# Bias rows of the second FFN as split bf16, residual loads on two queues, and a reordered entry of the first attention

## The chip, the cores and the metric

The kernel runs on one core of one Trainium2 chip. The metric is the device time of one execution in microseconds (us). TensorE is called PE here, VectorE DVE, ScalarE ACT, GpSimd POOL and SyncE SP, as in the profile.

## The reference

Six stages follow each other over a residual `x` of 8 batches x 512 tokens x 256 features, in float32:

```python
x = x + 0.5 * _L0_ffn_ref(_layernorm(x), ...)   # f0: 64 experts, top 3, capacity 128
x = x + _L0_attn_ref(_layernorm(x), ...)        # a0: windowed attention, window 32
x = x + 0.5 * _L0_ffn_ref(_layernorm(x), ...)   # f0
x = x + 0.5 * _L1_ffn_ref(_layernorm(x), ...)   # f1: 8 experts, all computed, top 2 weighted
x = x + _L1_attn_ref(_layernorm(x), ...)        # a1: causal attention
x = x + 0.5 * _L1_ffn_ref(_layernorm(x), ...)   # f1
```

The bias that the change touches is that of the second layer's FFN:

```python
y = jnp.einsum('bseh,ehd->bsed', h, W2) + b2
expert_out = jnp.einsum('bse,bsed->bsd', gate_full, y)
shared = jax.nn.gelu(x @ Ws1 + bs1, approximate=False) @ Ws2 + bs2
```

The sum over the experts of gate x `b2` is a product of its own: gates (tokens x 9, the ninth column is the shared expert's constant) times bias rows (9 x 256).

In a0, each pair of a token and one of its 32 window places gives a bond term and a damage term, both through a GELU; small 16x16 matrices (`w_state`, `w_strain`, ...) act on every head, and a mean over the window is taken with a banded matrix.

## The kernel before

The residual stays in SBUF as `x_resid`. `macaron` (L2692) runs `load_phase` and then the six stages; each stage is one block with a program per engine, and between stages all engines meet at a barrier (L51). A stage's first instructions therefore start about 1 us after the last engine has finished the stage before.

**Residual loads.** `load_x` (L54) issues eight DMAs of 512 KB, one per batch, on SP's queue: at the start of the kernel from `x`, and at the end of each f0 from the scratch `acc_rows` (L1576), once every expert's rows have been added (`y_added`). Each batch has a semaphore of its own (`wait_x`). After its loads `load_phase` writes zeros to scratch memory on the same queue (L88).

**Second FFN (f1, L186).** Per batch of 512 tokens, `up` (L293) makes the hidden layer of an expert (2 matmuls of 512 columns), ACT applies the GELU, `down` (L303) makes four token tiles of 256 columns, and DVE adds each tile, scaled by the gate, to the residual (`add`, L413). There are 9 such rounds n, one for each expert; four banks `y_ps` are used in turn, and `y_free` keeps PE from overtaking DVE by more than two rounds. Beside that, for the batch that follows: statistics at n = 0, normalised rows at n = 2, transposes at n = 4 and 5, gate logits at n = 6, and the gates themselves on DVE (`gates`, L381) at n = 7. At n = 2 PE turns the gates (9 rows) and DVE copies them to `gate_t` (L411). After the ninth round `biases` (L317) makes four matmuls with the 9 gate rows as weights and `b2_sb` (9 x 256, float32) as the moving side (L324); DVE adds the result as a tenth round. Before the loop over pairs of batches PE waits for `up_loaded` and `down_loaded` (L333), and DVE has computed `gates(0, 0)`. The biases are loaded by two DMAs (L257, L258).

**First attention (a0, L1712).** A batch is 16 chunks of 4 window places x 8 heads. For each chunk DVE makes `bond_buf` (`bond_chunk`, four instructions, L2411) and POOL `dmg_buf` (`damage_chunk`, L2062); ACT applies a GELU to each (L2336, L2341), PE reduces both. Three buffers of each kind are used in turn. Token work of the next batch is spread over the 16 steps. Only the first batch's token work and the matrices made of weights stand ahead of the loop; this is the entry that the change reorders. In the kernel before it runs as follows. SP issues 12 small loads (L1955 to L1963), then eight larger ones. DVE starts with the statistics of batch 0, waits for the small loads (L2575), spreads them with PE's help over heads (L2253, L2578, L2583), copies the transposed tokens (L2517) and goes on alternately with displacement tiles, the banded matrices (from L2606; they wait for POOL's constants, the last of which is an iota at L2052), statistics of the other batches, `split_bias` (L2498, seven small operations that turn the output bias into three bf16 rows), means, and the biases (`biases_ready`, L2632). PE makes q, a and c (L2237 to L2249) for the first half; `copy_c` (L2544) releases POOL's first chunk, and `bond_chunk(0)` ACT's first GELU.

Of the kernel before, what the change touches and what calls it, by code (L numbers as in the profile page):

```python
# [26 lines left out]
class Core:  # L27
# [26 lines left out]
    def load_x(self, sp, rows):  # L54
        for i in range(B):
            sp.dma_start(self.x_batch(i), rows[i * S:(i + 1) * S, :].rearrange("(j p) d -> p j d", p=P)).then_inc(
                self.x_loaded[i], 16)
        self.x_loads += 1
# [12 lines left out]
def load_phase(core, x_dram, scratch):  # L71
# [3 lines left out]
    with ExitStack() as ctx:  # L75
        zeroed = core.semaphore("zeroed")
        spare_zeroed = core.semaphore("spare_zeroed")
        block = ctx.enter_context(nc.Block())

        @block.sync  # L80
        def _(sp):
            core.load_x(sp, x_dram.rearrange("b s d -> (b s) d"))
# [9 lines left out]
        def _(pool):  # L92
# [6 lines left out]
                                    fill=1.0, base=0, pattern=[[-1, P]], channel_multiplier=1)  # L99

# [85 lines left out]
def ffn1_phase(core, name, gate_w, w1, b1, w2, b2, ws1, bs1, ws2, bs2, route_scale, out_dram=None):  # L186

    nc = core.nc  # L190
# [4 lines left out]
    YB = 4  # L195
    ctx = ExitStack()
    with ctx:
# [8 lines left out]
        b2_sb = sb("b2", [NE, D])  # L206
# [11 lines left out]
        gate_t = [sb(f"gate_t{k}", [NE, S]) for k in range(2)]  # L218
# [11 lines left out]
        const_ready = sem("const_ready")  # L230
        logits_ready = sem("logits_ready")
        sig_ready = sem("sig_ready")
        gate_ready = sem("gate_ready")
# [11 lines left out]
        def _(sp):  # L245
# [11 lines left out]
            sp.dma_start(b2_sb[0:E, :], b2).then_inc(down_loaded, 16)  # L257
            sp.dma_start(b2_sb[E:NE, :], bs2.rearrange("(o d) -> o d", o=1)).then_inc(down_loaded, 16)  # L258
# [7 lines left out]
        def _(pool):  # L266
            nc.gpsimd.iota(iota_e[:, :, :], pattern=[[0, TPB], [1, E]], base=0, channel_multiplier=0,
# [6 lines left out]
        def _(pe):  # L274
# [11 lines left out]
            def turn_gates(i, k):  # L286
                pe.wait_ge(gate_ready, i + 1)
                for j in range(TPB):
                    last = nc.tensor.transpose(gate_ps[0:NE, j * P:(j + 1) * P], gate[k][:, j, :],  # L289
                                               core.ident[:, :])  # L290
                last.then_inc(gate_t_ready, 1)
# [42 lines left out]
            pe.wait_ge(down_loaded, 64)  # L334
            with pe.Fori(0, B // 2) as pair:
                for k in range(2):
                    i = pair * 2 + k
                    for n in range(NE):
# [3 lines left out]
                        if n == 2:  # L342
                            turn_gates(i, k)
# [36 lines left out]
        def _(dve):  # L380
            def gates(i, k):  # L381
# [20 lines left out]
                for r in range(2):  # L402
# [4 lines left out]
                                        ALU.add).then_inc(gate_ready, 1)  # L407

            def copy_gates(i, k):
# [2342 lines left out]
```

## Time and profile before

| | |
|---|---|
| median of 3 runs | 3161.79 us (3155.25 to 3163.49) |
| the profiled execution | 3150.57 us, its span 3148.8 us |
| PE busy | 2839.0 us, 90% of the span |
| DVE / ACT / POOL busy | 53% / 49% / 41% |
| mean granted PE clock | 0.952 |

The stages can be told by their lines: f0 from 13 to 620 us and from 1339 to 1938 us, a0 from 629 to 1338, f1 from 1947 to about 2264 and from 2835 to the end, a1 in between. Read first the chain that ended last, for the stage at the end; then the busy time by stretches, for each stage's bound; then the timeline at the places that the change touches. A row of the timeline gives start, duration of the run of instructions, engine, line, operation, out<-in and count; in brackets stands the idle time ahead of it and what ended it. "issue" there is time in which the engine waited for nothing that the profile shows.

### The profile page before, as it was taken

How to read it: one execution, taken by the hardware profiler on the slowest of the kernel's cores; microseconds unless marked ns; L12 is line 12 of the kernel's file. 1: busy time of each engine (PE TensorE's matmuls, PEld its weight loads, DVE VectorE, ACT ScalarE, POOL GpSimd, SP SyncE). 2: the span in 40 equal slices, each digit the busy share in tenths (PEclk: the TensorE clock that was granted, in tenths of full speed). 3: DMA queues.
4: the chain of work that ended last, by engine and by line, in shares of the span. 5: the costliest groups of instructions: out<-in, count | busy, mean ns of one | idle time of the engine just before them, and what ended most of it. 6: DMA issues, size and time to landing. Idle time of an engine off the chain costs nothing. (4 is left out here: it accounts for less than half of the span.)

```text
span 3148.8 us, 54094 instructions
## 1 busy us (share of the span) xinstructions
PE 2839.0 (90%) x19481; PEld 2042.4 (65%) x19481; DVE 1666.4 (53%) x4549; ACT 1539.0 (49%) x2605; POOL 1306.5 (41%) x1303
## 2 busy tenths in 40 slices
PE   4899999758889988678999997999879999989999
PEld 3799999733344443358999996666546666655666
DVE  4411111178888888463111111666676666655666
ACT  1133333239999998311333332333257777772333
POOL 3544444349998889254444442000044444320000
PEclk9899999979999999868999998999989999998999
DMA  8199999711655555752999996000152344201000
GB/s 284 41 306 327 329 327 325 234 30 18 64 63 62 62 63 62 96 198 86 328 327 326 327 326 203 1 0 0 32 124 72 87 96 101 72 1 38 13 13 20
DMA packets 359857, 431.97 MB, mean 137 GB/s; under 512 B 86193, under 2 KB 314566, under 8 KB 356550
## 3 DMA queue, kind: packets, MB, share of 16 engines
q1 hardware_dynamic: 335046, 395.30, 45.5%
q0 software_dynamic: 24576, 33.57, 5.0%
q8 instruction: 144, 2.36, 0.3%
q14 instruction: 91, 0.75, 0.1%
HBM read 355.93 MB, written 72.88 MB: 136 GB/s over the span
## 5 line engine op out<-in xcount | busy, mean ns | idle before, releaser
L1675 ACT ACTIVATE f_h_t<-f_h_ps,f_b_t 128x128 f32<-128x128 f32 x1024 | 320.2, 364 | 596.3 <-PE f_h_ps L1633 596.3
L2062 POOL TENSOR_TENSOR a_dmg_buf<-a_c 128x2048 f32<-128x2048 f32 x128 | 520.1, 4091 | 85.2 <-DVE a_c L2544 42.7
L1633 PEld LDWEIGHTS f_h_ps<-f_rows_t,f_w 128*128 128x128 f32 x4096 | 481.4, 193 | 9.9 <-issue 3.5
L1633 PE MATMUL f_h_ps<-f_rows_t,f_w 128*128 128x128 f32 x4096 | 482.6, 276 | 2.3 <-DVE f_rows_t L1687 1.2
L1647 PE MATMUL f_y_ps<-f_w,f_h_t 128*128 128x256 f32 x2048 | 483.4, 379 | 0.0
L1593 POOL DMA_INDIRECT acc_rows<-f_y,f_give x128 | 205.1, 1603 | 487.2 <-DMA acc_rows<-f_y,f_give 451.6
L1647 PEld LDWEIGHTS f_y_ps<-f_w,f_h_t 128*128 128x128 f32 x2048 | 369.8, 190 | 39.9
L1687 DVE COPY f_rows_t<-f_t_ps 128x256 f32<-128x256 f32 x128 | 54.4, 425 | 598.4 <-PE f_t_ps L1621 593.7
L2411 DVE SCALAR_TENSOR_TENSOR a_bond_buf<-a_a,a_small_rep,a_q_ps 128x512 f32<-128x512 f32 x512 | 346.8, 740 | 5.3 <-PE a_q_ps L2238 2.2
L428 DVE SCALAR_TENSOR_TENSOR x_resid<-f_y_ps,f_gate,x_resid 128x256 f32 x512 | 218.8, 479 | 161.1 <-PE f_y_ps L311 155.5
L885 ACT ACTIVATE a_prob<-a_prob,a_neg_top 128x384 f32<-128x384 f32 (+3 forms) x512 | 276.5, 569 | 47.9 <-POOL a_neg_top L702 47.7
L299 PE MATMUL f_h_ps<-f_xn_t,f_w 128*128 128x512 f32 x584 | 282.8, 611 | 2.6 <-DVE f_xn_t L176 1.7
L998 DVE CUSTOM_DVE_ANT_0 a_prob<-a_s_ps,a_factor 128x384 f32<-128x384 f32 (+3 forms) x512 | 234.5, 486 | 87.5 <-PE a_s_ps L779 85.6
L360 ACT ACTIVATE f_h_t<-f_h_ps,f_b 128x512 f32<-128x512 f32 x146 | 100.3, 687 | 368.9 <-PE f_h_ps L299 368.6
L311 PEld LDWEIGHTS f_y_ps<-f_w,f_h_t 128*128 128x128 f32 x1152 | 220.1, 191 | 86.6 <-issue 53.7
L311 PE MATMUL f_y_ps<-f_w,f_h_t 128*128 128x256 f32 x1152 | 271.3, 381 | 0.1
L2336 ACT ACTIVATE a_bond_buf<-a_bond_buf,a_bond_act_b 128x2048 f32<-128x2048 f32 x128 | 255.7, 1998 | 16.5 <-DVE a_bond_buf L2411 12.2
L2341 ACT ACTIVATE a_dmg_buf<-a_dmg_buf,a_small_rep 128x2048 f32<-128x2048 f32 x128 | 255.0, 1992 | 0.0
L790 PE MATMUL a_t_ps<-ident,a_prob 128*128 128x128 f32 x1280 | 232.6, 281 | 17.0 <-ACT a_prob_t L896 13.3
L896 ACT COPY a_prob_t<-a_t_ps 128x512 f32<-128x512 f32 (+1 forms) x352 | 192.8, 548 | 100.6 <-PE a_t_ps L790 99.3
L702 POOL TENSOR_SCALAR a_neg_top<-a_top 128x1 f32<-128x1 f32 x512 | 105.8, 211 | 324.4 <-DVE a_top L998 307.1
L790 PEld LDWEIGHTS a_t_ps<-ident,a_prob 128*128 128x128 f32 x1280 | 145.5, 142 | 108.7 <-ACT a_prob L885 47.7
(337 smaller groups left out, 4110.4 us busy)
## 6 DMA issues: line engine op xcount, KB each, us to landing
f_w<-in_L_ffn_w_dram SPq DMA_DIRECT2D x256, 1024.0 KB
a_skewed<-skew SPq DMA_DIRECT2D x32, 512.0 KB, 7.2
a_k_s<-parts SPq DMA_DIRECT2D x16, 768.0 KB, 7.9
acc_rows<-x_resid SPq DMA_DIRECT2D x17, 512.0 KB, 5.3
xn_rows<-f_xn SPq DMA_DIRECT2D x16, 512.0 KB, 3.0
x_resid<-acc_rows SPq DMA_DIRECT2D x16, 512.0 KB, 8.3
a_vals<-val_rows SPq DMA_DIRECT2D x64, 128.0 KB, 4.2
skew<-a_bond SPq DMA_DIRECT2D x128, 64.0 KB
```

The source lines that it names most:

```text
L299: last = nc.tensor.matmul(h_ps[(k * NE + n) % 2][:, :], w1_sb[:, RUN[n], c, :], norm.xn_t[k][:, c, :], start=c == 0, stop=c == DC - 1)
L311: last = nc.tensor.matmul(y_ps[m % YB][:, j, :], h[:, t * P:(t + 1) * P], w2_sb[:, RUN[n], :], start=True, stop=True)
L790: last = nc.tensor.transpose(t_ps[pack % TB][:, col + kb * P:col + (kb + 1) * P], prob[:, u % PR, kb * P:(kb + 1) * P], core.ident[:, :])
L885: nc.scalar.activation(prob[:, u % PR, 0:width], prob[:, u % PR, 0:width], ACT.Exp, bias=neg_top[:, u % PR:u % PR + 1]).then_inc(exp_ready, 1)
L998: nc.vector.tensor_tensor_reduce(out=prob[:, u % PR, 0:width], in0=s_ps[use % SB][:, 0:width], in1=factor[:, S - width:S], scale=1.0, scal ...
L1633: last = nc.tensor.matmul(h_ps[n // HB][:, (n % HB) * P:(n % HB + 1) * P], w1_sb[s][:, c, n * P:(n + 1) * P], rows_t[e % 2][:, c, :], star ...
L1647: last = nc.tensor.matmul(y_ps[k][:, 0:D], h_t[k][:, n, :], w2_sb[e % R][:, n, :], start=n == 0, stop=n == HC - 1)
L1675: nc.scalar.activation(h_t[k][:, n, :], h_ps[n // HB][:, (n % HB) * P:(n % HB + 1) * P], ACT.Gelu, bias=b1_t[:, n, e:e + 1]).then_inc(gelu ...
L2062: nc.gpsimd.tensor_tensor(dmg_buf[n % RING][:, :, :], places(c_sb[h], first_place(dg)), c_sb[h][:, PAD:].unsqueeze(1).broadcast_to([P, DG, ...
L2336: nc.scalar.activation(buf[:, :, :], buf[:, :, :], ACT.Gelu, bias=bond_act_b[:, h:h + 1]).then_inc(bond_act, 1)
L2341: nc.scalar.activation(buf[:, :, :], buf[:, :, :], ACT.Gelu, bias=small_rep[:, B_DAMAGE:B_DAMAGE + 1]).then_inc(dmg_act, 1)
L2411: last = nc.vector.scalar_tensor_tensor(out=bond_buf[n % RING][:, dd, :], in0=a_sb[h][:, d + 1:d + 1 + S], scalar=small_rep[:, POS + d:POS ...
```

## The change

It has four parts.

1. **Second FFN's biases in bf16.** Each float32 bias value is split into three bf16 parts, and so is each gate; the products of every gate part with every bias part are made in one bf16 matmul with 96 rows (three blocks of 32, in each 3 x 9 used rows) in place of a float32 one with 9 rows. The biases are loaded nine times over (18 small DMAs in place of 2), behind a memset on POOL. `split_biases` (8 DVE operations) stands after `gates(0, 0)`, and PE waits for it ahead of its loop. Per batch DVE gets `split_first` (4 operations, n = 0) and `split_second` (2, n = 1); the gates are turned and copied at n = 3, from a single `gate_t` buffer.
2. **Residual loads on two queues.** SP loads the even batches, ACT the odd ones, in `load_phase` and at the end of each f0.
3. **The 12 small loads of a0** are issued in `load_phase`, between the residual loads and the writing of zeros.
4. **a0's entry.** On DVE and PE what depends on weights and constants alone comes first, the banded matrices and their wait for POOL's iota among it; then batch 0's statistics. `make_a` comes ahead of `make_q`, `inverse_std` ahead of `copy_c`; `split_bias` stands after `bond_chunk(0)`; ACT runs one GELU on a single column, right after the second square root.

```diff
+    def load_x(self, queue, rows, batches):
+        for i in batches:
+            queue.dma_start(self.x_batch(i), ...)
...
+        @block.scalar
+        def _(act):
+            core.load_x(act, x_dram.rearrange("b s d -> (b s) d"), range(1, B, 2))
         @block.sync
         def _(sp):
+            core.load_x(sp, x_dram.rearrange("b s d -> (b s) d"), range(0, B, 2))
+            attn0.load(sp)
             sp.wait_ge(spare_zeroed, 1)
...
+            sp.wait_ge(b2_cleared, 1)
+            for m in range(PARTS):
+                for l in range(PARTS):
+                    row = 32 * m + NE * l
+                    sp.dma_start(b2_sb[row:row + E, :], b2).then_inc(b2_loaded, 16)
+                    sp.dma_start(b2_sb[row + E:row + NE, :], bs2.rearrange("(o d) -> o d", o=1)).then_inc(b2_loaded, 16)
...
-                        last = nc.tensor.matmul(y_ps[m % YB][:, j, :], gate_t[k][:, t * P:(t + 1) * P],
-                                                b2_sb[:, :], start=True, stop=True)
+                        last = nc.tensor.matmul(y_ps[m % YB][:, j, :], gate_t[:, t * P:(t + 1) * P],
+                                                b2_rows[:, :], start=True, stop=True)
...
-            pe.wait_ge(down_loaded, 64)
+            pe.wait_ge(down_loaded, 32)
+            pe.wait_ge(b2_split, 1)
...
+            def split_biases():
+                dve.wait_ge(b2_loaded, 32 * PARTS * PARTS)
+                nc.vector.tensor_copy(b2_part[:, :], b2_sb[:, :])
+                nc.vector.drain()
+                nc.vector.tensor_copy(b2_rows[0:32, :], b2_part[0:32, :])
+                nc.vector.tensor_tensor(b2_rest[:, :], b2_sb[:, :], b2_part[:, :], ALU.subtract)
+                nc.vector.drain()
...
+            def split_first(k):
+                nc.vector.tensor_copy(gate_part[0][:, :, :], gate[k][:, :, :])
+                nc.vector.drain()
+                nc.vector.tensor_tensor(gate_rest[:, :, :], gate[k][:, :, :], gate_part[0][:, :, :], ALU.subtract)
+                nc.vector.tensor_copy(place_part(0), across(gate_part[0][:, :, :]))
+                nc.vector.drain()
+                nc.vector.tensor_copy(gate_part[1][:, :, :], gate_rest[:, :, :])
...
             gates(0, 0)
+            split_biases()
...
             sp.wait_ge(y_added, 16 * E)
-            core.load_x(sp, sparse.acc)
+            core.load_x(sp, sparse.acc, range(0, B, 2))
...
+            act.wait_ge(y_added, 16 * E)
+            core.load_x(act, sparse.acc, range(1, B, 2))
...
+            nc.scalar.activation(tanh[:, 0:1], core.ident[:, 0:1], ACT.Gelu)
...
             dve.wait_ge(bands_ready, 1)
...
+            bn_stats(0, 1)
+            aggregate(0, 1)
+            variances(0, 1)
+            inverse_std(0, 1, 1)
...
             copy_a(0, 0)
-            variances(1, B)
+            inverse_std(1, B, 2)
             copy_c(0, 0)
-            inverse_std(1, B, 2)
             dve.wait_ge(pads_ready, 1)
             bond_chunk(0)
+            split_bias()
             for s in range(LAST):
                 if s + 1 < CHUNKS:
                     bond_chunk(s + 1)
```

## Rows read from the trace of the kernel before

**Rows 1.** The chain that ended last, shares of the span by line:

```profile
by line: PE f_h_ps L299 4.1%; PE f_y_ps L311 3.9%; PE f_gate_ps L281 0.5%; PE f_y_ps L324 0.4%; PE f_tp L164 0.3%; PE f_gate_ps L289 0.1%; issue 0.1%; DVE x_resid L428 0.1%; DVE f_xn_t L176 0.0%; DVE f_xn L152 0.0%; DVEq L458 0.0%; DVE f_st
```

**Rows 2.** Busy us by stretch, a0's second batch: stretch, length, PE, PEld, DVE, ACT, POOL:

```profile
765.00:847.00 82.00, 69.41 (x574) 29.44 (x578) 71.57 (x113) 80.41 (x54) 78.97 (x21) 0.98 0.51 59
```

**Rows 3.** Timeline, PE: last f1's bias matmuls and what follows; two bf16 matmuls of a1:

```profile
2994.72 1.99 PE L324 MATMUL f_y_ps<-f_b,f_gate_t 9*128 9x256 f32 x8
2996.64 3.70 PE L299 MATMUL f_h_ps<-f_xn_t,f_w 128*128 128x512 f32 x8
...
2801.07 0.28 PE L777 MATMUL a_s_ps<-a_k_s,a_q_s 96*128 96x256 bf16 x1
2801.19 0.22 PE L779 MATMUL a_s_ps<-a_mask_b,a_ident_b 128*128 128x128 bf16 x1
```

**Rows 4.** Timeline, DVE, last f1: the adds at n = 2 and n = 8:

```profile
2971.92 1.74 DVE L428 SCALAR_TENSOR_TENSOR x_resid<-f_y_ps,f_gate,x_resid 128x256 f32 x4 [1.49 <-PE f_y_ps L311]
...
2996.93 1.66 DVE L428 SCALAR_TENSOR_TENSOR x_resid<-f_y_ps,f_gate,x_resid 128x256 f32 x4 [0.17 <-PE f_y_ps L324]
```

**Rows 5.** Timeline, entry of the last f1:

```profile
2841.96 0.25 SPq L258 DMA_DIRECT2D f_b<-in_L_ffn_bs_dram  x1
2850.51 3.76 PE L299 MATMUL f_h_ps<-f_xn_t,f_w 128*128 128x512 f32 x4
2854.36 2.87 PE L311 MATMUL f_y_ps<-f_w,f_h_t 128*128 128x256 f32 x8
2855.04 0.19 DVE L406 TENSOR_TENSOR f_gate<-f_part 128x32 f32<-128x32 f32 x1
```

**Rows 6.** Timeline, DVE: first and last of the seven operations of a0's `split_bias`:

```profile
656.47 0.27 DVE L2501 CAST a_b_out_part<-a_b_out 3x256 bf16<-3x256 f32 x1
...
658.81 0.47 DVE L2512 SCALAR_TENSOR_TENSOR a_b_out_rows<-a_ctx,ident,a_ctx_t 3x256 bf16<-3x256 f32 x1
```

**Rows 7.** Timeline, entry of the first f1:

```profile
1963.54 3.78 PE L299 MATMUL f_h_ps<-f_xn_t,f_w 128*128 128x512 f32 x4 [0.86 <-DMA f_b<-in_L_ffn_bs_dram]
1967.07 0.19 DVE L406 TENSOR_TENSOR f_gate<-f_part 128x32 f32<-128x32 f32 x1
```

**Rows 8.** Timeline, SP: first two and last of eight residual loads; a0's first load:

```profile
620.06 0.92 SPq L56 DMA_DIRECT2D x_resid<-acc_rows  x2
...
625.66 2.17 SPq L56 DMA_DIRECT2D x_resid<-acc_rows  x1
628.97 0.35 SPq L1955 DMA_DIRECT2D a_rel_t<-_L_attn_rel_pos_emb_dram  x1
```

**Rows 9.** Timeline, all engines, entry of a0:

```profile
631.86 2.07 ACT L2370 ACTIVATE a_xn<-x_resid,a_less_mean,a_rstd 128x256 f32<-128x256 f32 x4 [0.48 <-DVE a_less_mean L2567]
637.84 0.72 PE L2253 MATMUL a_o_ps<-a_small,a_select 16*128 16x85 f32 x2 [23.89 <-DVEq L2576]
638.25 0.24 POOL L2052 IOTA a_inv_count<- 128x128 f32 x1 [6.92 <-issue]
641.46 1.07 DVE L2517 COPY a_xn_t<-a_tok_ps 128x512 f32<-128x512 f32 x1
652.37 0.95 DVE L2610 RECIPROCAL a_inv_count<-a_inv_count 128x128 f32<-128x128 f32 x1
682.53 1.28 ACT L2336 ACT_TABLE_LOAD   x1 [8.97 <-DVE a_bond_buf L2411]
683.82 2.00 ACT L2336 ACTIVATE a_bond_buf<-a_bond_buf,a_bond_act_b 128x2048 f32<-128x2048 f32 x1
```

**Rows 10.** Timeline: two DVE operations beside work of POOL, and POOL's first chunks:

```profile
640.05 2.48 DVE L2588 COPY a_b_state<-a_small_rep 128x2 f32<-128x2 f32 x1
...
675.09 12.04 POOL L2062 TENSOR_TENSOR a_dmg_buf<-a_c 128x2048 f32<-128x2048 f32 x3 [32.59 <-DVE a_c L2544]
675.25 4.38 DVE L2567 SCALAR_TENSOR_TENSOR a_less_mean<-a_mean_var,a_rstd 128x28 f32<-128x28 f32 x1
```

**Rows 11.** Timeline, DVE, first f0: the wait for the gate bias:

```profile
24.67 0.18 DVE L1431 CAST f_gate_b_part<-f_gate_b 3x64 bf16<-3x64 f32 x1 [5.25 <-DMA f_gate_b<-in_L_ffn_gate_b_dram]
```

More of the change, by code:

```diff
@@ L52, in free_semaphores, with begin_load_x @@
         self.sems = []
-    def load_x(self, sp, rows):
-        for i in range(B):
-            sp.dma_start(self.x_batch(i), rows[i * S:(i + 1) * S, :].rearrange("(j p) d -> p j d", p=P)).then_inc(
+    def begin_load_x(self):
+        self.x_loads += 1
+    def load_x(self, queue, rows, batches):
+        for i in batches:
+            queue.dma_start(self.x_batch(i), rows[i * S:(i + 1) * S, :].rearrange("(j p) d -> p j d", p=P)).then_inc(
                 self.x_loaded[i], 16)
-        self.x_loads += 1
     def wait_x(self, eng, i):
@@ L99, in _, with __init__, load @@
                                     fill=1.0, base=0, pattern=[[-1, P]], channel_multiplier=1)
+class Attn0Small:
+    def __init__(self, core, ctx, w_state, w_state_i, w_state_j, w_strain, w_damage, w_bond, w_damage_out, b_state, b_strain,
+                 b_damage, rel_pos, w_pos):
+        nc = core.nc
+        BD = w_state.shape[0]
+        self.small = ctx.enter_context(nc.sbuf_tensor("a0_small", [BD, 5 * BD + 5 + WIN], FP32))
+        self.rel_t = ctx.enter_context(nc.sbuf_tensor("a0_rel_t", [BD, WIN], FP32))
+        self.w_pos_sb = ctx.enter_context(nc.sbuf_tensor("a0_w_pos", [BD, BD], FP32))
+        self.loaded = nc.alloc_semaphore("a0_small_loaded")
+        self.squares = (w_state, w_state_i, w_state_j, w_strain, w_damage)
+        self.columns = (w_bond, w_damage_out)
+        self.biases = (b_state, b_strain, b_damage)
+        self.rel_pos, self.w_pos = rel_pos, w_pos
+        self.loads = len(self.squares) + len(self.columns) + len(self.biases) + 2
+    def load(self, sp):
+        BD = self.w_pos.shape[0]
+        sp.dma_start(self.rel_t[:, :], self.rel_pos.rearrange("w d -> d w"),
+                     allow_slow_non_contiguous=True).then_inc(self.loaded, 16)
+        sp.dma_start(self.w_pos_sb[:, :], self.w_pos).then_inc(self.loaded, 16)
+        at = 0
+        for w in self.squares:
+            sp.dma_start(self.small[:, at:at + BD], w).then_inc(self.loaded, 16)
+            at += BD
+        for w in self.columns:
+            sp.dma_start(self.small[:, at:at + 1], w).then_inc(self.loaded, 16)
+            at += 1
+        for b in self.biases:
+            sp.dma_start(self.small[:, at:at + 1], b.rearrange("(d o) -> d o", o=1)).then_inc(self.loaded, 16)
+            at += 1
 class Norm:
@@ L195, in ffn1_phase @@
     YB = 4
+    PARTS = 3
+    PROWS = 32 * PARTS
     ctx = ExitStack()
@@ new lines, in _ @@
+            aggregate(0, 1)
+            variances(0, 1)
+            inverse_std(0, 1, 1)
+            bn_stats(1, 2)
+            for c in range(DC):
+                copy_tokens(0, c)
+            bn_stats(2, 3)
+            copy_disp(0, 0)
+            bn_stats(3, 4)
+            copy_disp(0, 1)
+            nc.vector.tensor_scalar(damage_b[:, :], damage_b[:, :], 0.5, None, ALU.mult)
+            nc.vector.tensor_scalar(bond_b[:, :], bond_b[:, :], -5.0, None, ALU.add)
+            nc.vector.tensor_copy(b_val_r[:, :, :, :], b_val_sb[:, :, :, :].rearrange("p h r d -> p r h d"))
```

167 lines of the change are left out of this document (88 added, 79 removed).

## The prediction

> **What bounds the kernel.** I read the chain of waits first, for the stage that ends last. In f1 it is almost all PE, the matmuls of `up` and `down` with 4.1% and 3.9% of the span, and the four bias matmuls have 0.4% of their own [rows 1]. What PE saves inside f1's loop is therefore saved from the end. The busy time by stretches comes next: in a steady batch of a0 ACT works 80.41 of 82 us, POOL 78.97, PE 69.41 [rows 2]. ACT is a0's bound once its first GELU has begun, so a0's end moves with its first GELUs and with nothing else. Last I read the timeline at the starts of a0 and f1, where one engine waits for another's first result. The sum is made against the profiled execution (3150.57 us); the median of the runs shown is 3161.79, 11.2 more, and I put that difference on top at the end.
>
> **1. Bias matmuls.** One batch's four, eight records of float32, start at 2994.72 and the next `up` at 2996.64: 1.92 us, of which I count 4 x 0.43 = 1.72 for one batch and 0.2 for the switch to the next shape. A bf16 matmul of 96 rows and 256 columns starts at 2801.07 and the next matmul at 2801.19, 0.12 later [rows 3]. The saving is 4 x (0.43 - 0.12) = 1.23 us per batch. It counts where PE sets the pace: at n = 2 DVE stood idle for 1.49 us because PE had not finished. In the batch whose tail comes after the gate chain DVE is the late one (0.17 idle at n = 8) [rows 4], and the phase's last batch ends on DVE's adds. So 7 batches of 8 count, 14 in both phases: -17.2 us. Bounds: if the weights' load (0.10, my estimate) does not hide behind the matmul, 0.22 each, -11.6; with all 16 batches and 1.27 each, -20.3.
>
> The loop also gets six DVE operations a batch, on 128x36 elements and fewer. The nearest row is an addition of 128x32 at 0.19 [rows 5], with a 0.05 wait for each drain, about 1.4 us in all, 0.85 at n = 0 and 0.55 at n = 1. The 1.49 us of idle time at n = 2 covers them, and the ring of four banks lets DVE lag by about a round beside. I take nothing. Without that cover each microsecond would count 14 times. The copy of the turned gates moves one round later with PE's turning, in the same cover, and its result is needed only after n = 8. Turning costs the same with 96 columns as with 9, the moving side being the identity's 128 columns.
>
> **2. Entry of the last f1.** PE now waits for `split_biases`, behind `gates(0, 0)` on DVE. That ends at 2855.23 [rows 5]. The split's eight operations on 96x256 are one more than a0's seven on 3x256, which ran from 656.47 to 659.28, 2.8 us [rows 6]. PE would start its loop at 2858.1 in place of 2850.51 [rows 5], 7.6 later, and gets back 0.4 between `up` and `down`: +7.2. The 18 small loads end their issue about 8 us after 2842.2 at 0.25 to 0.46 each (the row of a bias load, [rows 5]; the pace of SP's issues, [rows 8]), before the gates are ready; at 1.14 a pair they would add 1.8. Range +5 to +11.
>
> **3. Entry of the first f1.** Here the loop started at 1963.54, after waiting for the shared bias, while the gates ended at 1967.26 [rows 7]. The stage begins earlier by what the second queue saves (below, up to 5.8), but the weights queue behind the same traffic; of that I take 2.3. Gates at 1965.0, plus 2.9 for the split is 1967.9, less 0.15: +4.2. Range 2 to 8; 6.3 if the second queue gives nothing.
>
> **4. Start of a0.** SP issues the eight loads from 620.06 on, two in 0.92, but the last alone takes 2.17 and ends at 627.83; a0's own first load is at 628.97 [rows 8]. Four loads on a queue at 0.46 end at 622.0, and the stage begins at 623.2, 5.8 earlier. Whether they do hangs on what stalled the last issues: if it is the depth of one queue, four don't reach it; if the stall is common to both, nothing is gained. The two ends are 5.8 and 0, and I take 5.8, as the first two show no stall.
> The Trainium skill (DMA: Bandwidth & Descriptors, Issuing engines are not separate DMA queues) speaks against this part: issuing from several engines saves only the sequencer's time to issue. By that rule this step is still 5.8 if the 2.17 us is such time, and 0 if it is the DMA engines' backlog; no row separates them.
>
> **5. Order of a0's entry.** DVE now waits for POOL's constants ahead of everything that needs x. The last, an iota, started at 638.25 after 6.92 us for which the profile names no releaser, and ended 9.5 after the stage's first load [rows 8, 9]. Shifted by 5.8 that is 632.7; since that wait need not move with the start, I take 634.7 (632.5 to 638.5). Behind it on DVE stand the bands (2.2 with the reciprocal's 0.95 [rows 9]) and copies, 3.1 in all; then batch 0's statistics and its normalising, which took from 628.97 to 633.93, 4.96 [rows 8, 9]; then PE's turning, 1.2 (an estimate). The first copied tokens come at 643.9 in place of 641.46 [rows 9], +2.4. PE loses nothing by the small loads any more, for which it had waited 23.89 [rows 9], but that wait is no longer the last.
> From there to the first GELU it took 42.4 us [rows 9]. Off that go the table load of 1.28, made early [rows 9]; 4.2 for `less_mean`, which took 4.38 beside POOL's first chunk for 128x28 elements [rows 10] and now comes before it; and 3.6 for bands, `split_bias` and biases moved away and `make_a` made first (0 to 6: their 5 us and more partly filled DVE's waits for PE). That leaves 33.3: first GELU at 677.2 against 683.82, -6.6.
>
> **6. `split_bias` behind `bond_chunk(0)`.** It now runs while POOL makes its first chunks back to back, 12.04 for three [rows 10]. The row to look at is `less_mean`: a tiny operation whose inputs both lie in SBUF took 4.38, as long as POOL's chunk. A copy of 128x2 took 2.48 beside a POOL operation too [rows 10]. Where the split ran before, POOL was idle, and it took 2.8 [rows 6]. Let T be the start of POOL's first chunk. `bond_chunk(0)` takes 2.9 (from the end of `less_mean` at 679.63 to the table load at 682.53 [rows 9, 10]), the first GELU starts at T + 3.1, and the second bond GELU wants its chunk at T + 6.9. Undisturbed, DVE delivers it at T + 2.8 + 2.8 + 2.8, 1.6 late. If the seven operations wait until three chunks are over, 8.7 late; if a fourth slips in between, 13.8. I take 11. ACT has no slack to win it back [rows 2]. a0 in sum: -6.6 + 11 = +4.4, range -9 to +13.
> The Trainium skill (SBUF — State Buffer, Who interferes with whom) calls the shared port pair "an exclusive lock": a DVE operation with two SBUF inputs contends with a GpSimd operation that reads SBUF, and copies and casts in a 2-port mode with any. Rows 10 agree; by the rule in full all seven wait, 13.8, and the whole sum would be +2.0, 3163.8 us.
>
> **7. First f0.** The 12 small loads stand ahead of the zeros; f0's first vector work waited 5.25 for its gate bias anyway [rows 11]. +0.6, range 0 to 2.8.
>
> **Sum.** -17.2 + 7.2 + 4.2 + 4.4 + 0.6 = -0.8: 3149.8 profiled, 3161.0 on the median. That is no change; about 0.3% (9.5 us) is what a measurement of this kernel can tell.
>
> **Rivals.** A: POOL does not hold `split_bias`, because its chunks leave gaps or because operations on three partitions pass. Then 1.6 in place of 11: sum -10.2, 3151.6. Against it stand the two rows [rows 10]; for it, that they are two. Chance 0.27.
> B, slower: the two queues share what stalled SP, so the stage begins at 629 as before. It decides if the stage's first instruction is later than 628. DVE's wait for the iota then ends at 638.5 (+3.8), f1 starts at +6.3 (+2.1): sum +5.1, 3166.9; with a fourth chunk and a slow load of the biases 3172. Chance 0.2.
> C: the bf16 matmuls do not do what they should, since at 0.22 each and with 0.5 us of DVE's six operations uncovered per batch the loop wins 11.6 - 7. Sum +11.8, 3173.6. Against it is the idle time at n = 2 [rows 4]. Chance 0.08.
> My forecast has 0.45.
>
> **Chances.** Faster by over 0.3% needs below 3152.3: half of A, and A or the forecast with PE's full saving or an earlier a0, 0.28. Slower by over 0.3% needs above 3171.3: C, and the upper part of B, 0.15. Within: 0.57. The range goes from 3147 (A with -20.3 and 2 less at f1) to 3174 (C).
>
> **What the profile after would show.** Step 1: four bf16 matmuls on `b2_rows`, 0.5 us from first to next `up`; DVE still idle at n = 2. Steps 2 and 3: the first `up` of the loop starts 2.9 after the last gate operation, PE's wait ended by DVE. Step 4: the first instruction of a0 at 623 or 629. Step 5: DVE waits for POOL before the bands, first GELU near 677. Step 6: some of the split's operations take 2 to 4 us instead of 0.4, and ACT idles about 11 us before its third GELU; in case A it idles 1.6. The forecast fails above all if that gap is absent, or if PE, idle for longer ahead of f1's loop, is granted a clock well under the 0.98 of a steady stretch [rows 2] for longer than before.

## The result, and the profile after

| | before | after |
|---|---|---|
| median of 20 runs each | 3163.74 us | 3173.13 us |
| ratio to the kernel before | | 1.0026, 95% interval 1.0016 to 1.0037 |
| the profiled execution, its span | 3150.57, 3148.8 us | 3169.98, 3168.2 us |
| mean granted PE clock | 0.952 | 0.945 |

The change makes the kernel slower by 0.26%, some 8 to 9 us (8.2 by the ratio, 9.4 by the medians). No change to speak of was forecast (-0.8 us); the time lies inside the range, on its upper side. The two profiled executions differ by 19.4 us, more than the medians, because the first profile of the kernel before was one of its shorter executions, 13 us below its median; that is taken apart below.

The chain that ended last has the same form as before [rows 1], with the bias matmuls at 0.1% instead of 0.4%:

```profile
by line: PE f_h_ps L362 4.1%; PE f_y_ps L374 3.9%; PE f_gate_ps L344 0.5%; PE f_tp L207 0.3%; issue 0.1%; PE f_gate_ps L352 0.1%; PE f_y_ps L387 0.1%; DVE x_resid L526 0.1%; DVE f_xn_t L219 0.0%; DVE f_xn L195 0.0%; DVE f_top_i L454 0.0%; D
```

Since every stage begins at a barrier, the two traces can be laid side by side at a few marks, and the difference at each mark says where time was lost or won:

| mark | before | after | shift | step of it |
|---|---|---|---|---|
| first load of the first f0 | 13.31 | 18.63 | +5.3 | +5.3 |
| first residual load at its end | 620.06 | 623.97 | +3.9 | -1.4 |
| first load of a0 | 628.97 | 627.58 | -1.4 | -5.3 |
| first bond GELU | 683.82 | 687.95 | +4.1 | +5.5 |
| second bond GELU | 687.63 | 706.21 | +18.6 | +14.5 |
| last bond GELU | 1275.29 | 1302.19 | +26.9 | +8.3 |
| first residual load, second f0 | 1938.52 | 1965.50 | +27.0 | +0.1 |
| first load of the first f1 | 1947.50 | 1968.98 | +21.5 | -5.5 |
| its loop | 1963.54 | 1995.31 | +31.8 | +10.3 |
| first load of a1 | 2258.54 | 2284.15 | +25.6 | -6.2 |
| first load of the last f1 | 2835.49 | 2859.93 | +24.4 | -1.2 |
| its loop | 2850.51 | 2882.30 | +31.8 | +7.4 |
| last store of the output | 3144.96 | 3164.36 | +19.4 | -12.4 |

The largest single step is between the first two bond GELUs of a0. Timeline of ACT, after (start, duration, engine, line, operation; in brackets the idle time ahead and what ended it):

```profile
687.95 2.00 ACT L2431 ACTIVATE a_bond_buf<-a_bond_buf,a_bond_act_b 128x2048 f32<-128x2048 f32 x1 [8.57 <-DVE a_bond_buf L2508]
689.86 1.99 ACT L2436 ACTIVATE a_dmg_buf<-a_dmg_buf,a_small_rep 128x2048 f32<-128x2048 f32 x1
706.21 2.00 ACT L2431 ACTIVATE a_bond_buf<-a_bond_buf,a_bond_act_b 128x2048 f32<-128x2048 f32 x1 [14.37 <-DVE a_bond_buf L2508]
```

ACT, the stage's bound, waits 14.37 us for DVE's second chunk. This second chunk is the next `bond_chunk`, which stands behind `split_bias` on DVE. What DVE and POOL did meanwhile, after:

```profile
685.12 2.72 DVE L2508 SCALAR_TENSOR_TENSOR a_bond_buf<-a_a,a_small_rep,a_q_ps 128x512 f32<-128x512 f32 x4
687.76 2.08 DVE L2598 CAST a_b_out_part<-a_b_out 3x256 bf16<-3x256 f32 x1
689.92 3.88 DVE L2600 TENSOR_TENSOR a_ctx<-a_b_out,a_b_out_part 3x256 f32<-3x256 f32 x1
693.72 3.89 DVE L2601 TENSOR_SCALAR a_ctx_t<-a_b_out_part,ident 3x256 f32<-3x256 bf16 x1
697.69 4.43 DVE L2603 CAST a_b_out_part<-a_ctx 3x256 bf16<-3x256 f32 x1
702.19 0.41 DVE L2605 TENSOR_TENSOR a_ctx<-a_ctx,a_b_out_part 3x256 f32<-3x256 f32 x1
```
```profile
685.17 16.80 POOL L2156 TENSOR_TENSOR a_dmg_buf<-a_c 128x2048 f32<-128x2048 f32 x4 [40.36 <-DVE a_c L2641]
```

The first cast took 0.27 us in the kernel before [rows 6] and 2.08 here; three further operations took about one chunk of POOL each (16.80 / 4 = 4.2), and as soon as POOL's fourth chunk is over, at 701.97, the next runs in 0.41. `bond_chunk`, whose second input is in PSUM, ran beside POOL's first chunk in 0.68 a piece: it is not POOL's being busy, but what the operation reads and writes, that makes it wait.

The other large step is a0's entry. DVE, after:

```profile
640.83 4.07 DVE L2692 TENSOR_SCALAR a_inv_count<-a_inv_count 128x128 f32<-128x128 f32 x1 [9.26 <-POOL a_inv_count L2146]
644.98 0.95 DVE L2696 RECIPROCAL a_inv_count<-a_inv_count 128x128 f32<-128x128 f32 x1
647.14 1.40 DVE L2647 BATCH_NORM_STATS2 a_stats<-x_resid 128x6 f32<-128x256 f32 x4
```

and POOL, after:

```profile
640.56 0.24 POOL L2146 IOTA a_inv_count<- 128x128 f32 x1 [10.49 <-issue]
641.31 3.50 POOL L2174 MEMSET a_vals<- 128x4096 f32 x1
```

DVE waits 9.26 us for the iota. Its first operation behind it took 0.22 us in the kernel before and takes 4.07 here, up to 644.90, just past the end of POOL's memset at 644.81. Only then do the statistics of batch 0 begin, 19.6 us into the stage.

### The profile page after: what moved, and what is told of

Read it like the earlier page. It is cut to its first block and busy times, and to the rows that moved or that the text cites. A ratio compares the mean times of both kernels' runs of the same rounds, so it can differ in the third digit from the quotient of the medians.

```text
span 3168.2 us, 54169 instructions
## 1 busy us (share of the span) xinstructions
PE 2819.4 (89%) x19417; PEld 2029.3 (64%) x19417; DVE 1694.3 (53%) x4659; ACT 1538.5 (49%) x2606; POOL 1306.5 (41%) x1307
```

## The experiments

Ratios are to the kernel before, timed on the same chip in the same job, with 95% intervals. The kernel before had medians of 3162.9, 3167.4, 3173.4 and 3162.3 us in the four jobs of these experiments, so medians are set against each other only within a job: `after_again`, `split_early`, `bands_late` and `bias_wait_late` ran in the first; `iota_first`, `small_on_act` and `best` in the second; `bias_only` and `one_queue` in the third; `iota_f0` and `best_small_sp` in the fourth. A difference of two ratios below is uncertain by 6 to 7 us, more where a kernel ran six times or fewer. The last two columns are from each kernel's profile: from a0's first load (or, where no row of it is named, the stage's first instruction) to the first bond GELU, and from there to the second.

| kernel | median | ratio | to first GELU | to second |
|---|---|---|---|---|
| before, first profile | 3163.74 | 1 | 54.9 | 3.8 |
| before_again | 3164.25 (one run) | | 53.9 | 3.8 |
| after_again | 3172.90 | 1.0032 (1.0017 to 1.0046) | 60.3 | 18.3 |
| split_early | 3161.50 | 0.9988 (0.9973 to 1.0002) | 61.2 | 3.8 |
| bands_late | 3167.64 | 1.0009 (0.9993 to 1.0025) | 49.5 | 18.3 |
| bias_wait_late | 3161.62 | 0.9992 (0.9977 to 1.0006) | 57.1 | 18.3 |
| iota_first | 3178.47 | 1.0048 (1.0028 to 1.0068) | 59.0 | 18.3 |
| iota_f0 | 3173.93 | 1.0044 (1.0027 to 1.0062) | 48.6 | 18.3 |
| small_on_act | 3175.64 | 1.0034 (1.0018 to 1.0049) | 60.2 | 18.3 |
| bias_only | 3167.46 | 0.9981 (0.9964 to 0.9998) | 55.0 | 3.8 |
| one_queue | 3190.04 | 1.0059 (1.0037 to 1.0081) | 57.3 | 18.3 |
| best_small_sp | 3139.70 | 0.9938 (0.9922 to 0.9953) | 48.7 | 3.8 |
| best | 3137.00 | 0.9909 (0.9892 to 0.9926) | 49.0 | 3.8 |

**The changed kernel again.** No edit.

> The changed kernel once more, as it is, so that the others of this job can be set against it on one chip. Its profile differs from that of the kernel before by +19.4 us, its median by +9.4. Theory F: the entries and the split give what they gave in the first profile (first GELU of a0 60.4 us after the stage's first load, 18.3 us from the first to the second bond GELU, f1's loops starting 31.8 and 31.8 us later than before), and the 8 us that came up inside a0's loop do not come back, since they are waits for DMAs that differ from run to run. Rival R: they come back (at batches 1, 2 and 5, some 8 us in sum), and belong to the change.

1.0032, and the entry and the gap stand as they were (60.3, 18.3). From the second to the last bond GELU it took 600.0 us, as against 596.0 in the first profile and 587.7 in that of the kernel before. This alone favours the rival, so it needed a second profile of the kernel before.

**The kernel before again.** No edit.

> The kernel before once more, for a second profile of it. In its first profile a0 took 587.7 us from the second bond GELU to the last; in five profiles of the changed kernel and its variants it took 596.0 to 600.0. Theory F (DMA waits that differ from run to run, and a first profile that was a fast one, 13 us below its median): now 593 or more. Rival R (the change lengthens a0's loop by itself): 586 to 590 again.

It took 603.7 us from the second to the last bond GELU (681.02 to 1284.75), longer than both profiles of the changed kernel. One and the same kernel spans 587.7 to 603.7 in this stretch, and `bias_only` below, whose a0 is that of the kernel before, takes 612.1. The 8.3 us that came up there are thus no effect that these profiles can put down to the change; 587.7 is the shortest of all 14, the other 13 lie between 596.0 and 612.1. In the first f0 the kernels likewise took 602 to 613 us from first load to the residual's loads, without a pattern. Part of it shows in the trace: in the profile after, DVE once waits 4.28 us in this stretch for a releaser that the profile calls remote. The first profile of the kernel before has no such wait, the second has three, 9.6 us together, and the other profiles have one to four. What they wait for was not followed.

**The split of the output bias put back.**

```diff
             for h in range(HALF):
                 copy_disp_t(0, h)
+            split_bias()
             bn_stats(5, 7)
...
             bond_chunk(0)
-            split_bias()
```

> The changed kernel with split_bias put back to where POOL is idle, between the copies of the displacement tiles and the statistics of batches 5 and 6. Theory F (POOL's chunks hold each of the split's operations): the gap from the first to the second bond GELU falls from 18.3 to 3.8 us, the seven operations take 2.8 us, part of it in DVE's waits for PE, so the whole kernel is 12 to 14.5 us faster than the changed one, that is 3 to 5 us faster than the kernel before. Rival R (the gap comes of something else at the loop's start, such as DVE's instructions arriving late): the gap stays above 10 us and the time within 3 us of the changed kernel's.

The gap fell from 18.3 to 3.8 us and the ratio from 1.0032 to 0.9988, 14 us by the ratios and 11.4 by the medians. The next bond GELU now follows at once, as in the kernel before. The split, with POOL idle, in this kernel:

```profile
666.94 0.27 DVE L2598 CAST a_b_out_part<-a_b_out 3x256 bf16<-3x256 f32 x1
667.28 0.41 DVE L2600 TENSOR_TENSOR a_ctx<-a_b_out,a_b_out_part 3x256 f32<-3x256 f32 x1
667.62 0.34 DVE L2601 TENSOR_SCALAR a_ctx_t<-a_b_out_part,ident 3x256 f32<-3x256 bf16 x1
```

The same three operations take 1.02 us here and 9.85 in the changed kernel. Theory F holds, the rival does not. The placement of these seven operations alone costs about 14 us, more than the whole change loses.

**The bands behind the second displacement tile.**

```diff
             nc.vector.tensor_copy(state_t[:, :], dmg_ps[:, 0:P]).then_inc(state_t_copied, 1)
-            dve.wait_ge(bands_ready, 1)
-            nc.vector.tensor_scalar(inv_count[:, :], inv_count[:, :], float(WIN), None, ALU.min)
...
             bn_stats(3, 4)
             copy_disp(0, 1)
+            dve.wait_ge(bands_ready, 1)
+            nc.vector.tensor_scalar(inv_count[:, :], inv_count[:, :], float(WIN), None, ALU.min)
...
```

> The changed kernel with the wait for POOL's iota and the five operations on the banded matrices behind the second displacement tile, as in the kernel before; all else stays first. Theory F (the wait for the iota, 9.3 us, and POOL's long memset, which then held DVE for 3.9, are the price of the entry): batch 0's statistics start about 632.5 instead of 647 on the first profile's clock, the first GELU comes 10 to 13 us sooner, and the kernel is 10 to 13 us faster than the changed one. Rival R (the entry is bound by PE's chain of tokens, displacements and means, and the bands then stand in its way again): 3 to 6 us.

In the profile the first GELU comes 10.8 us sooner after the stage's start (60.3 to 49.5), as theory F had it. By the ratios the kernel wins 0.23%, 7 us, by the medians 5.3, each with an uncertainty of some 6; that lies between the two theories and decides for neither. What the entry wins is shown by its rows:

```profile
638.88 0.28 DVE L2690 COPY a_state_t<-a_dmg_ps 128x128 f32<-128x128 f32 x1
641.51 1.40 DVE L2647 BATCH_NORM_STATS2 a_stats<-x_resid 128x6 f32<-128x256 f32 x4
659.25 0.22 DVE L2714 TENSOR_SCALAR a_inv_count<-a_inv_count 128x128 f32<-128x128 f32 x1
```

The stage starts at 635.18 here, so the statistics begin at 6.3 us instead of 19.6, and the operation that took 4.07 takes 0.22, with POOL's memset long over.

**PE's wait for the split biases, moved into `biases`.**

```diff
             pe.wait_ge(down_loaded, 32)
-            pe.wait_ge(b2_split, 1)
...
             def biases(i, k):
+                pe.wait_ge(b2_split, 1)
```

> The changed kernel with PE's wait for the split biases moved from ahead of the loop into biases, where it is long fulfilled. Theory F: PE starts each f1 loop as soon as its weights are there, 7.4 us sooner in the last f1 and 4 to 5 in the first; DVE begins its adds 2.9 us later than in the kernel before, which the ring of four banks takes up. The kernel is 8 to 12 us faster than the changed one. Rival R: DVE, late by 2.9 us, holds PE through y_free, and what is gained is 12.2 - 5.8 = 6 us or less.

Ratio 0.9992, 12.7 us below the changed kernel by the ratios, 11.3 by the medians. The loop of the last f1 starts 15.0 us after the stage's first load instead of 22.4, as it did in the kernel before (15.0):

```profile
2875.41 3.42 PE L344 MATMUL f_gate_ps<-f_gate_w,f_xn_t 128*128 128x8 f32 x16
2878.68 3.76 PE L362 MATMUL f_h_ps<-f_xn_t,f_w 128*128 128x512 f32 x4
```

and from there to the last store it takes 282.6 us, as in the changed kernel (282.1). DVE's later start held nobody: the rival falls. In the first f1 the loop starts 24.2 us after the residual's first load, as against 29.8 in the changed kernel and 25.0 in the kernel before. The entry of a0 has the same code here as in the changed kernel and took 57.1 us instead of 60.3, so that stretch too varies by some 3 us from run to run.

**The iota ahead of POOL's memsets.**

```diff
+            nc.gpsimd.iota(inv_count[:, :], ...)
             nc.gpsimd.memset(diag[:, :, :], 1.0)
...
-            nc.gpsimd.iota(inv_count[:, :], ...).then_inc(bands_ready, 1)
```

The increment of `bands_ready` goes to the mask operation before it.

> The changed kernel with POOL's iota ahead of its memsets in a0 instead of behind its masks; the same instructions, one of them moved. The iota started 10.5 us late, with no releaser in the profile. Theory F (POOL waits for its further instructions there, whichever they are, while the residual's loads are under way): the iota runs in the stage's first microsecond, the idle time of 7 to 10 us stays in POOL's stream at about the same place and falls on the memset that comes there; DVE has its bands at once, and the first GELU comes 9 to 13 us sooner. Rival R (the iota itself needs something that takes 10 us to load): the idle time moves ahead of the iota, to the stage's start, everything of POOL is 10 us later, and the first GELU comes no sooner.

Here theory F fell and the rival held:

```profile
635.66 0.24 POOL L2126 IOTA a_inv_count<- 128x128 f32 x1 [16.19 <-issue]
635.86 0.19 POOL L2128 MEMSET a_diag<- 128x128 f32 x1
```

The stage starts at 625.3, and the wait moved with the iota to the front, 10.4 us of it inside the stage. It belongs to the iota, not to its place in POOL's stream. All masks came later, so DVE waited 10.88 us for one of them, and the first GELU came no sooner to speak of (59.0).

**One more iota at the end of f0.**

```diff
                 if e + R < E:
                     gather(e + R)
+            nc.gpsimd.iota(early_iota[:, :], ...)
```

> The changed kernel with one iota more, into a tile that nothing reads, at the end of POOL's work in each f0, behind its last indirect DMA. In all profiles the first iota after f0's experts waited 7 to 12 us, those after the first phase, a0 and the second attention not at all. Theory I (POOL pays some 10 us at the first iota behind indirect DMAs and broadcasts, wherever it stands): the added iota starts 10 us behind POOL's last DMA, that is at about 632 on the first profile's clock and so 4 us behind the end of the stage as it was; a0 starts 4 to 5 us later, its own iota runs without a wait, the first GELU comes 54 to 56 us behind the stage's first load instead of 60.3, and the time changes by less than 3 us. Rival J (the wait belongs to the new stage, its instructions or its loads): the added iota runs at once, a0's own waits as before, nothing changes.

```profile
618.08 1.55 POOL L1699 DMA_INDIRECT acc_rows<-f_y,f_give  x1 [2.94 <-DMA acc_rows<-f_y,f_give]
627.01 0.24 POOL L1719 IOTA f_early_iota<- 128x128 f32 x1 [7.38 <-issue]
...
633.93 0.23 POOL L2149 IOTA a_inv_count<- 128x128 f32 x1
```

Theory I: the added iota waits 7.4 us behind the last indirect DMA, and a0's own iota then has no wait. The stage begins 6 us later for it (631.48, where the residual's loads begin at 621.91; 3.6 us between the two in the changed kernel, 9.6 here), and the first GELU comes 48.6 us after the stage's start, less than the 54 to 56 expected. Counted from the residual's first load it comes 5.8 us sooner than in the changed kernel (58.15 for 63.98), and the loop of the first f1, ahead of which the same was done, 2.2 later (31.97 for 29.81). In time no gain can be seen: 1.0044 for 1.0032, each uncertain by some 5 us. So the first iota behind f0's indirect DMAs and broadcasts costs POOL 7 to 12 us, wherever it stands; in the profile it is idle time without a releaser. Whether the indirect DMAs or the broadcasts bring it about no run separates. The Trainium skill (GPSIMD Engine Reference, Instruction dispatch) says that the first call to a freshly loaded kernel of this engine pays a load of about 6 us, "with no visible profile instruction"; the rows agree in kind, and no run here shows the load itself.

**The small loads on ACT's queue.**

```diff
             core.load_x(act, ..., range(1, B, 2))
+            attn0.load(act)
...
             core.load_x(sp, ..., range(0, B, 2))
-            attn0.load(sp)
```

> The changed kernel with the 12 small loads of the first phase issued by ACT, behind its four residual loads, instead of by SP ahead of the zeros. Theory F (SP's issue time sets the end of the first phase; 12 loads take it 10.0 us, of which 5.3 showed at f0's start): SP is done at about 8.5, ACT at about 13.5, f0 starts at 14 instead of 18.6, and of these 4.5 us 2 to 4.5 reach the end. Rival R (the zeros' and residual's traffic, not the issue, sets f0's progress, whose gate bias lands no sooner): less than 1 us.

f0's first load came at 14.42 instead of 18.6, but the gate bias was used at 25.77 instead of 26.59, and the ratio is 1.0034 against 1.0032. By the ratio this run favours the rival. The rows favour a part of the theory. In the nine profiles that have the small loads on SP, the experts' first matmul comes at 145.8 to 151.1 (median 148.6) and the first f0 ends, at the residual's first load, at 621.0 to 631.5 (median 621.8); in the two that have them on ACT, this one and `best`, the matmul comes at 146.6 and 146.7 and the end at 620.1 and 619.0. Some 2 of the 4.2 us thus seem to reach the end of that stage, too little to show in the ratios.

**The biases alone, in the kernel before.**

```diff
-                        last = nc.tensor.matmul(y_ps[m % YB][:, j, :], gate_t[k][:, t * P:(t + 1) * P],
-                                                b2_sb[:, :], start=True, stop=True)
+                        last = nc.tensor.matmul(y_ps[m % YB][:, j, :], gate_t[:, t * P:(t + 1) * P],
+                                                b2_rows[:, :], start=True, stop=True)
...
+            pe.wait_ge(b2_split, 1)
...
+            split_biases()
```

> The kernel before with the first part of the change alone (split bf16 biases in the second FFN), its residual loads, small loads and a0 as before. Theory F: the two f1 loops get 6.2 and 12.4 us shorter and their entries 7.4 and 4 to 5 us longer, the first of these shorter by what the single queue leaves; in sum 5 to 8 us faster than the kernel before, ratio 0.998, with the same 1.4 us stall at the head of each pair of batches in one of the two loops if it belongs to the longer loop. Rival R (the loops' saving in the changed kernel came from elsewhere): the loops take 295 us as before and the kernel is 10 us slower.

The second FFN is that of the changed kernel, all else that of the kernel before. 0.9981, 6 us faster: taken alone, this part of the change wins, even with PE's wait ahead of the loop. The loops take 289.7 and 282.1 us instead of 295.0 and 294.5. The three stalls of 1.48 us in the first f1 (below, point 1) are there too, and in neither profile of the kernel before, so they come with this part. In this profile a0, whose code is that of the kernel before, is the slow one of the note on `before_again` (612.1 us), and the profiled execution, 3179.09, lies 12 us above the median.

**Residual loads on one queue again.**

```diff
             sp.wait_ge(y_added, 16 * E)
-            core.load_x(sp, sparse.acc, range(0, B, 2))
+            core.load_x(sp, sparse.acc, range(B))
...
-            act.wait_ge(y_added, 16 * E)
-            core.load_x(act, sparse.acc, range(1, B, 2))
```

> The changed kernel with all eight residual loads at the end of each f0 back on SP's queue. Theory F (SP's issue of the last loads sets the stage's end, and a queue of four does not stall): a0 and the first f1 start 5.3 and 5.5 us later, behind loads that take 7.8 us to issue. In a0 the iota's own delay counts from POOL's start, so all 5.3 come through; in f1 the weights land 3 to 5 us later. The kernel is 8 to 11 us slower than the changed one, ratio 1.006 to the kernel before. Rival R (the transfers themselves set the first use of the residual and weights): 0 to 3 us slower.

```profile
621.72 8.96 SPq L59 DMA_DIRECT2D x_resid<-acc_rows  x8
631.82 0.37 SPq L2058 DMA_DIRECT2D a_w_disp<-in_L_attn_w_disp_dram  x1
```

From the first residual load to the stage's first it takes 10.1 us instead of 3.6; the ratio rises from 1.0032 to 1.0059, 0.27% or 8.6 us. By the ratios the second queue is worth 9 us, uncertain by some 8. By the rows it is less: of the 6.5 us by which a0 begins later here, 3.5 reach the first GELU (67.4 us after the residual's first load, 64.0 in the changed kernel), and the loop of the first f1 starts 1.3 us later against the same mark (31.1 for 29.8). The expectation that all 5.3 us come through in a0 was not met. The rival of a common queue falls: four loads a queue do not stall, with 2.25 us for all four of SP in the changed kernel.

**All four edits, and all but the last.**

> The changed kernel with four edits at once: split_bias where POOL is idle, the bands behind the second displacement tile, PE's wait for the biases in biases, the 12 small loads on ACT. Theory F (each price stands on the path by itself): -11.4 - 5 to -11 - 11.3 - 2 to -4 as the runs of one edit each gave or let expect, that is 30 to 37 us faster than the changed kernel and 20 to 27 us (0.6 to 0.9%) faster than the kernel before. Rival R (they overlap, one hides the other): less than 22 us below the changed kernel, within 0.4% of the kernel before.

> The version with four edits without the fourth: split_bias where POOL is idle, bands late, PE's wait in biases, but the 12 small loads on SP again, ahead of the zeros. It settles what f0's earlier start is worth. Theory F (f0's start reaches the end): 4 us slower than with all four, ratio 0.992 to the kernel before. Rival R (f0 is paced by its loads from then on): the same as with all four, 0.991. The first GELU of a0 comes 49 us behind its first load either way.

With all four the kernel takes 0.9909 of the time of the kernel before: 29 us by the ratio, 30 by the medians; by the ratios it is 39 us faster than the changed one. Without the small loads on ACT it is 0.9938. The profile with all four, ACT at a0's start:

```profile
661.76 1.28 ACT L2476 ACT_TABLE_LOAD   x1
...
671.51 2.00 ACT L2431 ACTIVATE a_bond_buf<-a_bond_buf,a_bond_act_b 128x2048 f32<-128x2048 f32 x1 [8.25 <-DVE a_bond_buf L2508]
673.42 1.99 ACT L2436 ACTIVATE a_dmg_buf<-a_dmg_buf,a_small_rep 128x2048 f32<-128x2048 f32 x1
675.31 1.99 ACT L2431 ACTIVATE a_bond_buf<-a_bond_buf,a_bond_act_b 128x2048 f32<-128x2048 f32 x1
```

The GELUs follow each other without a gap, and the first comes 49.0 us into the stage. The two ratios of this pair lie 0.29% apart, 9 us, twice what f0's earlier start can give (4.7 us), and their intervals overlap; the two ran in different jobs, and their own medians are 2.7 us apart. The pair of the changed kernel and the one with the small loads on ACT lies 0.02% apart. So it is open in the time how much of that start reaches the end. The three other edits add up within the noise: 14 + 7 + 13 us by their ratios, and 30 together.

## Why the prediction was wrong, point by point

It said that five terms cancel, -17.2 against +16.4. All of them were there, but of those that cost time the entry of a0, the split and the first f0 were priced too low, by 6.8, 3.5 and 2.7 us, and they decide the sign. The step that failed most is the first half of step 5.

**1. Bias matmuls: right in sum, -18.6 for -17.2.** A group of four now starts at 2277.65 and the next `up` at 2278.09:

```profile
2277.65 0.60 PE L387 MATMUL f_y_ps<-f_b_rows,f_gate_t 96*128 96x256 bf16 x4
2278.09 1.88 PE L362 MATMUL f_h_ps<-f_xn_t,f_w 128*128 128x512 f32 x4
```

That is 0.44 us for 1.92 [rows 3], 1.48 saved per batch and not 1.23: the 0.2 us I took for a switch of shape went as well. My lower bound set a weights' load of 0.10 beside each matmul, a figure from no row; at 0.11 for a whole matmul no such load shows. The loop of the last f1 got 12.4 us shorter, which is more than eight batches of 1.48; that only seven of eight count was not borne out, and the sum came out near by an offset. The loop of the first f1 got only 6.2 shorter: PE lost 4.4 in three stalls that I had not foreseen, and 1.8 more are not accounted for. At the head of a pair of batches DVE is late by 1.40 with no releaser shown, ACT's square root follows it, and PE waits for the GELU behind that:

```profile
2075.34 0.69 DVE L520 SCALAR_TENSOR_TENSOR x_resid<-f_y_ps,x_resid 128x512 f32 x1 [1.40 <-issue]
2078.08 0.21 ACT L187 ACTIVATE f_std<-f_var_eps 128x4 f32<-128x4 f32 x1 [4.12 <-DVE f_var_eps L182]
2080.41 1.99 PE L374 MATMUL f_y_ps<-f_w,f_h_t 128*128 128x256 f32 x8 [1.49 <-ACT f_h_t L424]
```

DVE's six new operations a batch took 0.8 and 0.4 us, no more than I gave them, and stayed hidden, as argued.

**2 and 3. Entries of f1: right.** +7.4 for +7.2 in the last, and in the first +4.8 for +4.2 (its loop against the residual's first load). In three of the nine profiles with the wait ahead of the loop, `after_again` among them, it is +5.6 in the last instead. There the 16 gate matmuls took 1.85 us, at a granted clock of 1.00 (2.4 GHz), where in the first profile after they took 3.42 at 0.50 (1.2 GHz):

```profile
2871.69 3.42 PE L344 MATMUL f_gate_ps<-f_gate_w,f_xn_t 128*128 128x8 f32 x16
```

My sign of failure, that PE after a longer idle time would be granted less, did not come: over 8 us from the start of the loops it was 0.70 and 0.73, in the kernel before 0.65 and 0.68. PE stood idle for 7.19 and 7.91 us, until the last operation of the split. The loads of the biases took 6.0 us to issue and were hidden in the last f1; in the first the split waited 0.62 for them.

**4. Start of a0: right.** 5.3 us for 5.8, and 5.5 in f1; one_queue undoes it. The rule of the Trainium skill (DMA: Bandwidth & Descriptors, Issuing engines are not separate DMA queues) that issuing from several engines saves issue time alone agrees with these runs: it was issue time that set the stage's start.

**5. Order of a0's entry: wrong by 6.8.** I had the first GELU 6.6 us sooner, counted from the residual's first load; it came 0.2 later (63.98 for 63.76). The failing step is the first half, from the stage's start to the first copied tokens: 25.7 us instead of my 20.7. The iota was ready 13.2 us into the stage, not 11.5, which is 1.7. From there to the statistics it took 6.3 us, not 3.1: the first operation behind the iota stood 3.9 us longer than by itself, up to the end of POOL's memset, which I had left out of the sum, though a copy of 128x2 that took 2.48 us beside work of POOL was among my own rows [rows 10]. The rest of that half took 6.1 us for 6.2. The second half was right: 34.7 us to the first GELU for 33.3, though part of its 33.3 rested on an estimate (3.6 for work moved away) and the same code took 32.0 in bias_wait_late. A run to run spread of 3 us leaves most of the 6.8 standing: `after_again` has 63.96 us from the residual's first load to the first GELU, and `before_again` 61.98. The choice that was wrong in kind is where I looked for the wait: I treated the iota's 6.92 us as a fixed lateness, when the question to ask was what the new place of the wait holds up. In the kernel before nobody had waited for it.

**6. `split_bias` behind the first chunk: right mechanism, mis-sized.** 14.5 us for 11, above my upper bound of 13.8. The first four operations each waited for a chunk of POOL to end, four chunks in all, and the last three ran undisturbed. Of the two prices I had, that of the Trainium skill (SBUF — State Buffer, Who interferes with whom), by which all such operations wait, was the better one: 13.8, and +2.0 for the sum. I took a value between it and a milder case for which no row spoke. Rival A, that POOL does not hold the split, had a chance of 0.27 against two rows that contradicted it; that was too much.

**7. First f0: wrong by some 3.** +3.3 at the experts' first matmul (146.5 to 149.8) for +0.6. The 12 loads took SP 10.0 us to issue, 2.01 and 2.86 for the first two, and the stage began 5.3 later. I set all of this against DVE's wait of 5.25 for the gate bias [rows 11]; but the bias is loaded by the same queue behind them, so the wait shrank by 3.4 and no more:

```profile
26.59 0.18 DVE L1535 CAST f_gate_b_part<-f_gate_b 3x64 bf16<-3x64 f32 x1 [1.85 <-DMA f_gate_b<-in_L_ffn_gate_b_dram]
```

DVE thus begins 1.9 us later than before; where the other 1.4 up to the first matmul come from was not followed, and that mark lies between 145.8 and 151.1 in the nine profiles with these loads on SP, between 143.2 and 146.5 in the three with f0 as before. How much of it arrives at the end is the open question above.

The measured terms give -18.6 + 7.4 + 4.8 + 0.2 + 14.5 + 3.3 = +11.6 us, and the medians are 9.4 apart, the ratio 8.2. Rival B (+5.1, nothing from the second queue) came near the time for a wrong reason: the queue gave its 5 us at both places. Rival C did not occur, since the bf16 matmuls and DVE's operations did what they should; that its 3173.6 us is the measured time almost to the digit is luck.

## What to carry to other kernels

Before small vector operations are moved off a path, look at what the other engine on the shared ports does at their new place: seven operations of 0.3 to 0.5 us cost 14.5 us beside GpSimd's long ones, because each of the first four waited for the end of one, and nothing beside an idle GpSimd. When a wait is moved forward in an in-order queue, price what now stands behind it, not how long it lasted where nobody needed it. And a result that a loop needs only at its end should be waited for there: one line moved gave back 11 to 13 us.

## What the runs showed of the hardware

- An engine's idle time without a releaser can belong to one kind of instruction. The first iota behind a stage with indirect DMAs and broadcasts waited 7 to 12 us in each of the 14 profiles, at the front of the stage (10.4 in iota_first) as behind twelve other operations (10.49 in the first profile after); behind other stages it ran at once.
- A DVE operation on 3 partitions x 256 elements waited for a GpSimd operation on 128 x 2048 (4.2 us) to its end, whether it was a cast, a tensor_scalar or a tensor_tensor on SBUF (2.08 to 4.43 us); a scalar_tensor_tensor on 128x512 with one tensor in PSUM did not (0.68).
- With six more operations on DVE in the loop body came a stall of 1.40 us at its head on DVE, three times in one of two instances of the same code, and none in the other; all 12 profiles with those operations have PE's three stalls of 1.48 us behind it, and neither of the kernel before. Why was not found.
- Two executions of one kernel differed by 16 us in a0's loop alone. A single profile's total is not good for less than that, but some of its steps are: the gap of 18.3 us came out at 18.26 to 18.29 in all eight profiles that had it.
